# A graph layer on one core: gathers limited to three in flight, and twenty tiles written to the output row by row

## The reference

```python
def _L0_gnn_ref(feat, efeat, W_msg, b_msg, W_attn, b_attn, src, dst):
    w_m = (efeat @ W_msg + b_msg).reshape(E, in_f, -1)
    w_a = (efeat @ W_attn + b_attn).reshape(E, in_f, -1)
    h_src = feat[src][:, :, None]
    e1 = w_m * h_src
    e2 = w_a * h_src
    seg_max = jax.ops.segment_max(e2, dst, num_segments=N)
    ex = jnp.exp(e2 - seg_max[dst])
    denom = jax.ops.segment_sum(ex, dst, num_segments=N)
    attn = ex / denom[dst]
    ft = jax.ops.segment_sum(e1 * attn, dst, num_segments=N)
    return ft.sum(axis=1)
...
x = _layernorm(x + _L0_gnn_ref(x, edge_attr_16, ..., src, dst), axis=-1)
x = _layernorm(x + _L1_gnn_ref(x, edge_index, edge_attr_16), axis=-1)   # mean of edge_attr by target
```

## Time and profile before

| quantity | value |
|---|---|
| median of 3 runs | 2309.12 us (2309.01 to 2309.82) |
| the profiled execution | 2309.43 us |
| its span, first to last instruction | 2307.6 us |
| mean granted TensorE clock | 0.946 |
| share of the chain that ended last: PE / POOL / issue / DVE | 36% / 30% / 14% / 14% |
| DMA, mean over the span | 20 GB/s, 46.93 MB |

### The profile page before, as it was taken

The page is one execution under the profiler, slowest core; times in us unless marked ns, Lnnn a source line. Parts: engine busy times, 40 slices in busy tenths (PEclk is TensorE's granted clock), DMA queues, the critical chain, the costliest instruction groups (busy, mean ns, idle before and its releaser), DMA issues.

```text
span 2307.6 us, 21909 instructions
## 1 busy us (share of the span) xinstructions
PE 2005.4 (87%) x6784; PEld 911.8 (40%) x6784; DVE 1867.7 (81%) x2922; ACT 1306.8 (57%) x1241; POOL 1682.1 (73%) x1748
## 2 busy tenths in 40 slices
PE   2548889998999998899989898899989898998886
PEld 0313334443444444444444443344444443444432
DVE  5557777987888988888987887798878887888886
ACT  6425545655566556665655755565556565565552
POOL 5777777777777777777777777777777777777740
PEclk8758999999999999999999999999999999999998
DMA  6100011001100001000100110101001010110110
GB/s 232 55 13 13 13 15 19 7 13 18 13 12 13 13 13 17 12 12 13 17 12 12 17 12 12 17 12 16 12 12 16 12 15 12 15 15 11 14 27 9
DMA packets 60072, 46.93 MB, mean 20 GB/s; under 512 B 28526, under 2 KB 55679, under 8 KB 59436
## 3 DMA queue, kind: packets, MB, share of 16 engines
q0 software_dynamic: 57776, 29.87, 9.3%
q1 hardware_dynamic: 2172, 15.58, 1.9%
HBM read 44.01 MB, written 1.23 MB: 20 GB/s over the span
## 4 chain that ended last, share of the span: by engine, by line
PE 36%; POOL 30%; issue 14%; DVE 14%; DMA 2%; ACT 2%; POOLq 0%; DVEq 0%; SPq 0%; ACTq 0%
POOL AR L624 29%; PE PX L1048 28%; PE PW L1034 7%; DVE AR L1348 7%; DVE AR L1361 3%; PE PTB L1023 2%; DVE AR L1378 1%; DMA AR<-in_xt,AR 1%; POOL AR L642 1%; DVE AR L1365 1%; POOL y_d L657 1%; DMA AR<-in_dst,QI 1%; ACT PX L881 0%; DVE AR L1379 0%; DMA AR<-in_es,AR 0%
## 5 line engine op out<-in xcount | busy, mean ns | idle before, releaser
L624 POOL DMA_INDIRECT AR<-in_xt,AR x1628 | 1572.2, 966 | 501.0 <-issue 486.6
L1048 PE MATMUL PX<-AR,CS 128*128 128x512 f32 x3304 | 1583.4, 604 | 6.8 <-ACT AR L825 6.6
L1348 DVE CUSTOM_DVE_ANT_1 AR<-PW,AR 128x1024 f32<-128x1024 f32 x826 | 987.7, 1220 | 183.0 <-PE PW L1034 127.6
L1048 PEld LDWEIGHTS PX<-AR,CS 128*128 128x128 f32 x3304 | 633.7, 193 | 586.5 <-issue 462.6
L1034 PE MATMUL PW<-WS,LT 100*128 100x512 bf16 x1652 | 514.8, 398 | 204.0 <-DVE AR L1348 203.0
L1361 DVE TENSOR_TENSOR AR<-AR,PX 128x1024 f32<-128x1024 f32 (+1 forms) x448 | 508.2, 1134 | 74.3 <-ACT PX L881 47.7
L819 ACT ACTIVATE LT<-PTB 100x1024 bf16<-100x1024 bf16 (+1 forms) x224 | 214.3, 957 | 529.8 <-PE PTB L1023 529.8
L883 ACT ACTIVATE AR<-AR 128x2048 f32<-128x2048 f32 (+1 forms) x224 | 429.3, 1917 | 7.3
L887 ACT ACTIVATE PX<-AR 128x1024 f32<-128x1024 f32 (+1 forms) x224 | 217.2, 970 | 326.4 <-DVE AR L1361 323.6
L1034 PEld LDWEIGHTS PW<-WS,LT 100*128 100x128 bf16 x1652 | 144.9, 99 | 584.2 <-issue 290.0
L881 ACT ACTIVATE PX<-AR 128x1024 f32<-128x1024 f32 (+1 forms) x224 | 235.6, 1052 | 22.9 <-DVE AR L1361 21.3
(11 more groups left out here) (149 smaller groups left out, 481.8 us busy)
## 6 DMA issues: line engine op xcount, KB each, us to landing
AR<-in_xt,AR POOLq DMA_INDIRECT x1631, 2.3
AR<-in_ea SPq DMA_DIRECT2D x3, 3128.0 KB, 13.6
AR<-in_ea SPq DMA_DIRECT2D x1, 3120.0 KB, 10.2
AR<-in_es,AR POOLq DMA_INDIRECT x49, 3.5
y_d<-AR POOLq DMA_INDIRECT x49, 2.1
AR<-y_d SPq DMA_DIRECT2D x1, 784.0 KB, 4.6
CS<-in_cst SPq DMA_DIRECT2D x1, 442.0 KB, 5.1
AR<-in_xt SPq DMA_DIRECT2D x1, 392.0 KB, 3.1
```

Source lines behind the costliest of these rows:

```text
L624: g.indirect_dma_start(feat(h, j - j0, j - j0 + 1), None, xt, bass.IndirectOffsetOnAxis(ap=XE[:, at:at + 1], axis=0)).then_inc(hg_sem(h), 16)
L1048: i = pe.matmul(PDR, IDN, x, start=(a == 0 and j == 0), stop=(g == LAST[k] and j == n - 1))
L1348: v.tensor_tensor_reduce(em(g, j, j + 2).rearrange("p (x c) -> p x c", c=32), w, hb, 1.0, LOW, ALU.mult, ALU.max, accum_out=MXC[:, k % 2, ...
```

## The change

1. **Three gathers in flight.** The gathers take three semaphores `d_h[0..2]` in turn, and gather x first waits until gather x-3 has landed. Whoever waits for gathers waits for all three semaphores (`landed`).
2. **MAIN goes from 46 to 29.** Only tiles 0 to 28 go through `y_d`; the other 20 tiles (REST) are written into `out` by rows, in batches of 12, 6 and 2. SP's reload waits for 29 results. DVE's norms of all nodes are cut into 14 pieces (`main`), one a step, in steps 166 to 179. POOL fetches the 20 tiles' own rows of x, and norms batches 0 and 1 with operations of its own (2 times 26 and 2 additions each, each waiting for the one before), then issues the row writes. DVE norms the last batch.
3. `y_d` is zeroed by one plain DMA on SP, issued after the first edge list has landed and ahead of the feature loads, in place of three indirect writes; `out` rows of tiles 29 to 48 therefore read zeros there.
4. **Head.** The sort's tables OH, DGC, QFR, KF, PK and a copy of the positions move from SBUF to PSUM. POOL loads tile 0's edge list before the run of targets, not behind it. The feature loads wait for that edge list, read a transposed copy of the input (`eat`) and are squared in unit stride; ACT's counts stand ahead of the squares. The sort's product runs ahead of the last overflow check. Two memsets move from POOL to DVE.
5. **Drain.** For the consumed groups 218, 221, 222 and 223 DVE adds pairs of slots first (`pairs`), which leaves PE 6 slots of 8.
6. The ring of weights has 64 slots, not 66; the list of steps is the same.

```diff
-MAIN = NC - 3
+MAIN = NC - 20
+REST = NC - MAIN
+BATCH = [(0, 12), (12, REST - 2), (REST - 2, REST)]
...
+        def landed(e, g):
+            n = UPTO[g]
+            for i in range(FLIGHT):
+                e.wait_ge(d_h[i], 16 * ((n - i + FLIGHT - 1) // FLIGHT))
...
             def gather(k, h):
-                j0, n = GRP[h][1:3]
-                for j in range(j0, min(j0 + n, CAPS[k])):
+                j0, n = GRP[h][1], SLOTS[h]
+                for j in range(j0, j0 + n):
+                    x = UPTO[h] - n + j - j0
+                    if x >= FLIGHT:
+                        g.wait_ge(d_h[x % FLIGHT], 16 * (x // FLIGHT))
...
+            sp.wait_ge(d_xe[0], 16)
+            sp.wait_ge(S["g_m"], 9)
+            sp.dma_start(YD.rearrange("(p c) w -> p c w", c=NC), OUTR[:, :, :]).then_inc(S["d_yz"], 16)
             features(0)
-            sp.wait_ge(d_xe[0], 16)
+            sp.wait_ge(S["d_yz"], 16)
             features(1)
...
-                sp.wait_ge(S["d_y"], 16 * NC)
+                sp.wait_ge(S["d_y"], 16 * MAIN)
...
                 for k in range(1, NC):
                     feats(k)
-                    if k >= 5:
+                    if 5 <= k < MAIN + 5:
                         results(k - 5)
...
+                    row_sums(y)
+                    then(g.tensor_scalar(s0, s0, -1.0 / 16, None, ALU.mult))
+                    then(g.tensor_tensor(y, y, s0.unsqueeze(2).broadcast_to([128, hi - lo, 16]), ALU.add))
+                    then(g.tensor_tensor(q, y, y, ALU.mult))
+                    row_sums(q)
...
+                for b, (lo, hi) in enumerate(BATCH):
+                    if hi < REST:
+                        g.wait_ge(S["a_out"], MAIN + hi)
+                        then(g.tensor_tensor(YS[:, lo:hi, :], YS[:, lo:hi, :], OUTR[:, MAIN + lo:MAIN + hi, 0:16], ALU.add))
+                        norm(lo, hi)
+                        then(g.tensor_tensor(YS[:, lo:hi, :], YS[:, lo:hi, :], means[:, lo:hi, :], ALU.add))
+                        norm(lo, hi)
+                    else:
+                        g.wait_ge(S["v_ys"], 1)
...
+                def main(x):
                     if x == 0:
...
                         v.wait_ge(S["d_xn"], 16)
                         v.wait_ge(S["d_yl"], 16)
                         link(v.tensor_tensor(XNN, XNN, YN[:, :, 0:16], ALU.add))
...
-                    if 0 <= i - USED[LAST[MAIN]] - 2 < 4:
-                        norms(i - USED[LAST[MAIN]] - 2)
+                    if 0 <= i - USED[LAST[MAIN - 1]] - 5 < 14:
+                        main(i - USED[LAST[MAIN - 1]] - 5)
```

More of the change, by code:

```diff
@@ L84 @@
 FROM.append(len(PAIR))
-RING = 66
+RING = 64
 AT, OLD, at, held = [], [], 0, []
@@ L136, with KEPT, gnn_kernel @@
 HMS = [x + 1 for x, seg in enumerate(SEGS) for g in seg]
+FLIGHT = 3
+SLOTS = [max(0, min(n, CAPS[k] - j0)) for k, j0, n, a in GRP]
+UPTO = [sum(SLOTS[:g + 1]) for g in range(NGR)]
 FINS = {USED[LAST[k]]: k for k in range(NC)}
 NST = len(STEPS) + 4
-def gnn_kernel(nc, xt, dst, src, ea, es, wc, cst, cst2, out):
+ADDS = [c for p, c in STEPS[-8:] if p is None]
+def KEPT(n):
+    return (n + 1) // 2
+def gnn_kernel(nc, xt, dst, src, ea, eat, es, wc, cst, cst2, out):
     f32, bf16, i32 = mybir.dt.float32, mybir.dt.bfloat16, mybir.dt.int32
@@ L357, in gnn_kernel @@
         STI = spare[:, 16 * NC:19 * NC].bitcast(i32).rearrange("p (x c) -> p x c", c=NC)
[L358 to L361, removed]
+        STS = spare[:, 19 * NC:19 * NC + 3 * REST].rearrange("p (x c) -> p x c", c=REST)
+        SSI = spare[:, 19 * NC:19 * NC + 3 * REST].bitcast(i32).rearrange("p (x c) -> p x c", c=REST)
+        YS = CS[:, 128:128 + 16 * REST].rearrange("p (c w) -> p c w", w=16)
+        SQS = YN[:, 0:REST, 0:16]
+        YB = YN[:, :, 0:16]
         SUF = sb("SUF", [128, HB])
@@ L638, in runs_of @@
                         g.wait_ge(S["a_p"], 4 * (k - 3) + 3)
-                        for h in range(FIRST[k - 3], LAST[k - 3] + 1):
-                            g.wait_ge(hg_sem(h), hg_count(h))
+                        landed(g, LAST[k - 3])
                     lo = xoff[k % 3]
@@ L988, in _, with check @@
             pe.wait_ge(S["v_id"], 1)
-            for q in range(NQE):
+            def check(q):
                 n = min(QE, EC - QE * q)
@@ L1327, in floors @@
                     k, j0 = GRP[lo][0:2]
-                    for g in range(lo, hi):
-                        v.wait_ge(hg_sem(g), hg_count(g))
+                    landed(v, hi - 1)
                     if lo == FIRST[k]:
@@ L1361, in gm, with pairs @@
                     v.tensor_tensor(y, y, EXP[:, 0:16 * w].rearrange("p (x o) -> p x o", o=16), ALU.mult).then_inc(S["v_gm"], 1)
+                def pairs(g):
+                    half = GRP[g][2] // 2
+                    keep = KEPT(half)
+                    v.wait_ge(S["a_exp"], g + 1)
+                    v.wait_ge(S["v_gm"], 2 * g + 2)
+                    sums = em(g, half, 2 * half - keep)
+                    v.tensor_tensor(sums, sums, em(g, half + keep, 2 * half), ALU.add).then_inc(S["v_ad"], 1)
                 def mean(k):
@@ L1497, in general @@
                 v.wait_ge(d_xe[0], 16)
-                for h in range(SOON):
-                    v.wait_ge(hg_sem(h), hg_count(h))
+                landed(v, SOON - 1)
                 for g5 in range(10):
@@ L1802 @@
     eap = np.concatenate([ea, np.zeros((EP - E, 16), ea.dtype)])
+    eat = np.concatenate([eap.reshape(128, EC, 16)[:, lo:lo + EC // NQE + 1].transpose(0, 2, 1).reshape(128, -1)
+                          for lo in range(0, EC, EC // NQE + 1)], 1)
     srcp = np.concatenate([src, np.zeros(EP - E, src.dtype)])
```

297 lines of the change are left out of this document (161 added, 136 removed).

## The result

The changed kernel takes 2332.57 us (median of 4 runs, 2331.86 to 2333.88) against 2309.47 of the kernel before: ratio 1.0098, 95% interval 1.0081 to 1.0116, 23 us slower. The forecast said slower, 2383 us, with a range of 2338 to 2415 (its sum has 2340 as the lower end once). The sign is right; the size is three times too large and the time lies 5 us under the range.

A forecast was written before the change was run, and what follows sets the result against it. POOL's gather issue was taken to bound the second half, with compute eating gathers as they land. Terms 86.2 + 5 - 18 + 8 - 7 + 3 - 1 - 2 = +74 gave 2383 us, range 2338 to 2415.

The forecast's parts named there:

- The reload in step 166: Before tile 31's first product DVE waits for `d_yl`, behind POOL's write after tile 33's gathers: 86.2 us lost.
- What it gives back: Tiles 31 to 47: with gathers stored, 472 slots take 1.266 us each instead of 1.304: -18 us.
- The bound of 1.188: Tiles 31 to 47: us a slot if PE alone decided, making the time given back -55 us.
- Clock restart: After the stall PE runs ten us at half speed: +5 us.
- `main` in 14 pieces: DVE's norm operations moved from the tail to steps 166 to 179, partly hidden: +8 us, between 0 and +18.
- The tail: From M, tile 48's first product, to the end: POOL's operations at 0.4 us end the kernel, M+82.4 against M+89.4: -7.
- `pairs`: In the drain, takes two of eight f32 slots from PE in four groups: -2 us, 0 to -4.
- The head: Kernel start: limit of three +18 us, earlier first gather -11, tables in PSUM -8; together -1, between -10 and +12.
- The limit in steady state: Gathers waiting for x-3 nearly always find it landed: +3 us, between 0 and +13.
- A: Rival: compute lags enough at tile 31 that the reload comes in time; about 2304 us, chance 0.07.
- B: Rival: waits for landings lengthen every gather's pitch, 0.04 us costing 50 us; about 2430 us, chance 0.08.
- C: Rival: the limit of three does nothing; 2362 to 2380 us, counted within the stall case's 0.85.

The follow-up runs named there:

- hold31_b: The kernel before, with DVE waiting ahead of tile 31's first product for tile 33's gathers and nothing else changed: 2329.28 us, ratio 1.0081.
- late13_f8_b: The changed kernel with `main` 13 steps later and eight gathers in flight instead of three: 2281.69 us, ratio 0.9880 against the kernel before.
- late13_b: The changed kernel with `main` 13 steps later, nothing else changed: 2312.32 us, ratio 1.0009 against the kernel before.

## Why the prediction was right or wrong

- *The reload in step 166*: right. Forecast 86.2 us, measured 84.1 of wait and +84.8 at tile 31, by exactly the chain named: POOL's write of tile 28's rows behind tile 33's gathers, then SP, then the landing.
- *What it gives back*: this is the step that failed. "I take 1.266 because it was measured with DVE, ACT and PE sharing the work as here." It was not as here. Measured without the change's edits (hold31_b): 1.181 a slot with the restart in it, 58 us repaid where -18 and +5 stood. In the changed kernel the forecast's stretch from tile 31 to tile 48 was -5 (+5, -18, +8) and came out at -48.7. Three signs against the 1.266 stood in the rows or close to them. First, DVE's floors waited 60.4 us for gathers; all of that goes once gathers are stored, and it is the size of what came back. Second, the stretch from 700 to 1100 us has a mean clock of 0.97: three of its eight pieces of 50 us have 0.90 to 0.93, each with one stop of PE of 2.9 or 3.0 us in it. Third, those are tiles of 34 to 38 slots, used for tiles of 24 to 30; PE did 2.04 f32 sums a slot there, and 1.96 in tiles 31 to 47. Two neighbouring pieces (PE alone, the kernel before):

```profile
850.00:900.00 50.00, 44.22 (x155) 0.93 0.10 14
900.00:950.00 50.00, 49.63 (x166) 1.00 0.10 13
```

  The stretch was read as a mean, and the second row shows compute without such a stop. The bound of 1.188 was no bound: it is PE's busy time with the half-clock time in it, and PE's own work came out at 1.138 in hold31_b. Why PE has more idle time beside the larger tiles was not isolated.
- *Clock restart*: +5 forecast, about 7 by the windows; in hold31_b the clock is back some 11 us after PE works again, about 5. *`main` in 14 pieces*: +8 forecast; the changed kernel's 9.5 us over hold31_b hold it and the longer restart.
- *The tail*: -7 (and -2 for `pairs`) forecast, -13.4 measured. POOL's operations cost 0.36 us, not 0.4, and tile 46's result was ready at M+36.7, not M+40. That the sum with 0.4 came near is partly luck: the 0.36 is a mean over operations of many sizes with their gaps. The Trainium skill, "GPSIMD Engine Reference", section "4.1 Engine selection", puts two-input operations at about twice VectorE's time; like for like this case shows less, 0.28 to 0.30 us on POOL for 48 elements a partition against 0.21 on DVE for 49, 1.4 times.
- *The head*: each term right. First gather at 19.43 us (forecast near 21), the limit's cost 17.2 us (18), and no gather beside DVE stretched: mean 943 ns from 19 to 91 us against 1177. In late13_f8_b, where the gathers follow as closely as before, the mean is 957, with one of 53 stretched (1.66 us at 82). So the tables in PSUM did end nearly all the stretches. The Trainium skill, "SBUF — State Buffer", section "Who interferes with whom", reports that such a DVE operation was not seen to stall a DMA that GpSimd issues; this case's 2.81 us beside one differs, and the measurement decides. Net: tile 28's last gather 3.0 us earlier than before, forecast -1.
- *The limit in steady state*: +3 forecast. From tile 0's last gather to tile 33's the changed kernel took 1.9 us more than the kernel before. Over the whole kernel it is 10.8 in late13_b, still within the bounds of 0 to 13.
- *Rivals*: A did not come (DVE did wait). late13_b is A's world, brought about on purpose: 2312 where A said 2304, since the limit takes 11 us in steady state and not 3. B was small: the mean gap before a gather stays near 0.31 us. C did not hold: the limit took 17.2 us in the head.
- *The range and the sum*: by stretch, the forecast had +88.2 up to tile 31 (86.2, 3 and -1), -5 to tile 48 and -9 behind it; measured are +84.8, -48.7 and -13.4. With -58 in place of -18 alone the forecast would be 2343, inside the range; the other differences of 3 to 4 us, all downward, put the time below it (the median of the runs is 2332.6). The lower bounds written down (-37 for the give-back, -10 and -8) reach 2328 together. The range was cut short of that on the ground that the terms do not all fall one way; here they did.

## What to carry to other kernels

A stall of a consumer costs its length only if nobody else bounds the kernel. Here the producer kept issuing, and each slot behind the stall repaid the difference between the producer's pitch (1.304 us) and the consumer's own rate (1.181), 0.12 us. So price a stall as its length minus the slots left times that difference; the waits of the consumer for the producer in that stretch (59.4 us here) say how much there is to win back. Take the consumer's rate from a stretch with the same shapes and the same share of work behind it. One place of the stall was tested, tile 31; the hold at tile 15 that should have tested the rule again gave no answer. A limit on transfers in flight that looks slack by the median landing still costs where transfers are slow (17 us beside the feature loads) and in the tail of the landings (11 us over 1600 gathers).

## What the runs showed of the hardware

POOL's elementwise operations of 6 to 96 elements a partition take 0.20 to 0.38 us with 0.08 us between dependent ones (54 in 19.7 us), but two of them took over 1.1 us. With eight gathers in flight a gather that waits for a landed one has the usual 0.30 us before it (34 rows); with three the 52 such gaps average 0.33, the longest 0.7. A PE that stood for 86 us ran some 15 us at half its clock afterwards, one that stood for 78 us some 11, and fed nearly without a gap it had 1.00 from 1912 to 2254 us. And one kernel on one chip took 2310 us on one occasion and 3200 on another, with PE standing still 40 times for nothing that the trace shows; what differed between the occasions was not found.
